# The last feature block of an adapter-conditioned attention and feed-forward layer: its second half leaves as 384 and 128 tokens where it left as 256 and 256

## The chip, the core and the metric

The program runs on one core of one Trainium2 chip. TensorE multiplies matrices (its weight loads are listed apart, as PEld), VectorE (DVE), ScalarE (ACT) and GpSimd (POOL) work on elements, and SyncE (SP) issues most transfers; a transfer issued from SP or ACT runs on the core's 16 DMA engines. Results of TensorE go to PSUM, eight banks of 128 partitions by 512 float32 columns; everything else lives in SBUF. The metric is the time of one execution in microseconds (us), lower is better, given as the median of three runs.

## The reference

32 batch entries of 32 tokens with 256 features, so 1024 tokens. Each batch entry picks one of eight adapters.

```python
x = x + attn(cond(x, itok, weights, fside), W_qkv, b_qkv, W_out, b_out)      # 16 heads of 16, causal
x = x + ffn(cond2(x, Wg, Wu, Wd, Ag, Bg, Au, Bu, Ad, Bd, itok), W1, W2, W3)

# cond2: _lora_linear(x, W, A, B, i) = x @ W + (x @ A[i]) @ B[i], hidden width 1024
h = silu(_lora_linear(x, Wg, Ag, Bg, i)) * _lora_linear(x, Wu, Au, Bu, i)
y = _lora_linear(h, Wd, Ad, Bd, i)

# ffn, hidden width 1024
hidden = silu(y @ W1.T) * (y @ W3.T)
hidden = fwht(hidden)                     # Walsh-Hadamard transform over the 1024
out = hidden @ W2.T                       # 1024 -> 256 features
```

Everything is float32. What the change touches is the last line, `hidden @ W2.T`, and the residual sum behind it.

## The kernel before

Activations are kept with features on the partitions and tokens along the free dimension: 1024 tokens are two halves of 512 (`HT`), and 256 output features are two blocks of 128 (`DC`). A float32 product is made of three fast ones: each operand is split into a high part, rounded to the short-mantissa kind `float32r`, and the rest, `lo`. The helper `both` (lines 480 to 489) issues the three matmuls for one block of 128 by 128 weights: weights high by activations high (L484), weights high by activations low (L486), weights low by activations high (L488). With two tiles given it does each of the three for both of them. Every matmul comes with its own load of 128 columns of weights. Where a small product can do without the split (conditioning, scores, adapters), plain float32 operands are used, in one instruction (L503, L558, L584, L613, L641, L681).

The stages follow each other on TensorE in an order written out by hand: conditioning, attention, the gated adapters' layer ("gate" and "up", then "d0" and "d1"), the feed-forward's two inputs ("f1" and "f3"), and the output product "w2". The Walsh-Hadamard transform has been folded into W2 on the way (`w2_hi`, `w2_lo`), so the last product reads the gated hidden state `h_hi`, `h_lo` directly.

The last stage stands at lines 802 to 813. The list `OUTS` (line 104) says in which pieces the output is made; each entry is (feature block, half of the tokens, first column, last column). The pieces are taken in the groups `[0, 1], [2], [3], [4]`. For a group, TensorE goes over `k`, the eight blocks of 128 hidden features (`HC`), and does the three matmuls of `both` for each, so that a group of one piece is 24 matmuls, each as wide as the piece. Pieces 0 to 2 are full halves of 512 tokens; pieces 3 and 4 share the last half of the last feature block. Each piece has a PSUM bank of its own (`psum_tiles`), freed long before.

When a piece's last matmul is done, VectorE adds the residual to it and writes `tmp_b` (lines 1333 to 1336), and SP, which does nothing else by then, sends that part of `tmp_b` to memory (lines 457 to 460); at the end it waits for all five transfers. Semaphores tie the three together: `full` from TensorE to VectorE, `out_made` from VectorE to SP, `out_stored` from the transfers to SP.

Of the kernel before, what the change touches and what calls it, by code (L numbers as in the profile page):

```python
# [46 lines left out]
HT = TOK // HALVES  # L47
# [53 lines left out]
           + [(PACKED_AT[n] + k * COLS, 1, COLS) for n in (P_D0, P_D1) for k in range(2)]  # L101
           + [(PACKED_AT[P_F + m], 1, COLS) for m in range(HC)])

OUTS = [(0, 0, 0, HT), (0, 1, 0, HT), (1, 0, 0, HT), (1, 1, 0, HT // 2), (1, 1, HT // 2, HT)]
WARM_UP = 14
ALONE = 6
KEEP_WARM = 7
# [21 lines left out]
def psum_tiles():  # L129
# [8 lines left out]
    last = [(a, s, m) for m in range(HC) for a in ("f1", "f3") for s in range(HALVES)]  # L138
    last += [("w2", j, 0) for j in range(len(OUTS))]
    bank_of = dict(plan)  # L140
# [24 lines left out]
def build(nc, index, first, x_slots, w_stream, matrices, w2_t, x_feat, out):  # L165
    with ExitStack() as ctx:
# [219 lines left out]
        def _(sp):  # L386
# [3 lines left out]
            def load_weights(n):  # L390
                if n >= STAGES:
                    wait_weights(sp, n - STAGES)
                at, runs, step = SOURCES[n]
                sp.dma_start(raw[:, n % STAGES, :].rearrange("p (a n) -> p a n", a=runs),
                             w_stream[:, at:at + runs * step].rearrange("p (a n) -> p a n", a=runs)[:, :, 0:COLS // runs])\
                  .then_inc(raw_loaded[n % STAGES], 16)
# [58 lines left out]
            for m in range(HC):  # L455
                load_weights(W_F + m)
            for j, (m, s, c0, c1) in enumerate(OUTS):
                sp.wait_ge(out_made, j + 1)
                sp.dma_start(out[m * P:(m + 1) * P, s * HT + c0:s * HT + c1], tmp_b[:, min(j, 3), c0:c1])\
                  .then_inc(out_stored, 16)  # L460
            sp.wait_ge(out_stored, len(OUTS) * 16)


        @block.tensor
        def _(pe):
# [14 lines left out]
            def both(tiles, w, xs, start, stop):  # L480

                last = []
                for ps, (x_hi, _) in zip(tiles, xs):
                    pe.matmul(ps[:, :], w[0], x_hi, start=start, stop=False)  # L484
                for ps, (_, x_lo) in zip(tiles, xs):
                    pe.matmul(ps[:, :], w[0], x_lo, start=False, stop=False)  # L486
                for ps, (x_hi, _) in zip(tiles, xs):
                    last.append(pe.matmul(ps[:, :], w[1], x_hi, start=False, stop=stop))  # L488
                return last
# [313 lines left out]
            for js in ([0, 1], [2], [3], [4]):  # L803
                tiles = [claim("w2", j, 0) for j in js]
                for k in range(HC):
                    pe.wait_ge(prod_split, ORDINAL["f3", 1, k] + 1)
                    m = OUTS[js[0]][0]
                    w = (w2_hi[:, k, m * P:(m + 1) * P], w2_lo[:, k, m * P:(m + 1) * P])
                    xs = [[h[s][:, k, c0:c1] for h in (h_hi, h_lo)] for _, s, c0, c1 in (OUTS[j] for j in js)]
                    outs = [ps[:, c0:c1] for ps, (_, _, c0, c1) in zip(tiles, (OUTS[j] for j in js))]  # L810
                    last = both(outs, w, xs, k == 0, k == HC - 1)
# [731 lines left out]
```

## Time and profile before

| | us |
|---|---|
| median of 3 runs | 214.09 |
| lowest and highest run | 214.02, 214.77 |
| the profiled execution | 214.37 |
| its span in the trace | 212.6 |
| TensorE busy | 206.2 (97%) |
| VectorE busy | 96.7 (45%) |

The span runs from the first to the last recorded event; the rest of an execution's time, here 1.77 us, lies around it. An engine's busy time counts its own instructions. Matmuls overlap, so the duration of one is longer than the time after which the next one starts; what a row of many matmuls costs is read from their starts. In the trace a plain float32 matmul leaves two matmul records and two load records, a `float32r` one leaves one of each; both kinds are called f32 in the rows, and they are told apart by their line.

### The profile page before, as it was taken

What the parts mean: (1) busy time and instruction counts of PE and PEld (TensorE: products, weight loads), DVE (VectorE), ACT (ScalarE), POOL (GpSimd) and SP (SyncE); (2) the same over time, 40 slices, a digit from 0 to 9 for tenths busy, and PEclk for the clock granted to TensorE, in tenths of its full rate; (3) what the DMA queues carried; (4) which work ended last, traced back from release to release, by engine and by line L of the source; (5) the groups of instructions that cost most, each with busy time, mean ns of one, the idle gap of its engine ahead of it and who ended that gap; (6) DMA issues with size and microseconds to landing.
All of it is one profiled execution on the core that took longest, in us unless ns stands there. A gap on an engine that the chain in (4) does not pass through costs nothing.

```text
span 212.6 us, 5689 instructions
## 1 busy us (share of the span) xinstructions
PE 206.2 (97%) x2265; PEld 164.8 (78%) x2265; DVE 96.7 (45%) x175; ACT 93.1 (44%) x162; POOL 104.9 (49%) x120
## 2 busy tenths in 40 slices
PE   7799999899999999999999999999999999999994
PEld 3467788588777878787888788788888888888894
DVE  3799998897557973020220300067922222220211
ACT  2356889585957042351450460324666664420000
POOL 4005788269656340827643458002599999440000
PEclk9999999999999999999999999999999999999999
DMA  5950056726430362041210451201011000000211
GB/s 152 393 209 3 5 143 159 208 57 173 116 90 15 91 189 74 0 114 24 62 29 23 122 233 33 69 0 33 19 49 54 0 0 0 0 3 0 99 49 49
DMA packets 16265, 16.68 MB, mean 78 GB/s; under 512 B 1776, under 2 KB 13040, under 8 KB 15984
## 3 DMA queue, kind: packets, MB, share of 16 engines
q1 hardware_dynamic: 15808, 15.26, 23.5%
q10 hardware_dynamic: 432, 1.07, 1.6%
q8 instruction: 18, 0.29, 0.6%
q14 instruction: 7, 0.06, 0.1%
HBM read 15.27 MB, written 1.05 MB: 77 GB/s over the span
## 4 chain that ended last, share of the span: by engine, by line
PE 88%; DVE 3%; DMA 3%; ACT 3%; issue 1%; SPq 0%; ACTq 0%
PE bank L484 25%; PE bank L486 23%; PE bank L488 23%; PE bank L641 8%; DMA raw<-w_stream 3%; PE bank L681 2%; DVE aux_lo L1144 1%; PE bank L558 1%; PE bank L584 1%; ACT k_x L843 1%; PE bank L613 1%; PE bank L503 1%; ACT aux_hi L878 1%; PE bank L539 1%; PE bank L538 1%
## 5 line engine op out<-in xcount | busy, mean ns | idle before, releaser
L1391 POOL TENSOR_TENSOR h_lo<-tmp_b,h_hi 128x512 fp32r<-128x512 f32 x32 | 42.6, 1353 | 40.7 <-ACT h_hi L892 40.7
L484 PE MATMUL bank<-act_hi,w_hi 128*128 128x512 f32 x144 | 52.7, 402 | 0.1
L486 PE MATMUL bank<-act_lo,w_hi 128*128 128x512 f32 x144 | 51.1, 391 | 0.0
L488 PE MATMUL bank<-act_hi,w_lo 128*128 128x512 f32 x144 | 50.9, 389 | 0.0
L1214 DVE TENSOR_TENSOR tmp_b<-bank,tmp_a 128x512 f32<-128x512 f32 x32 | 20.7, 684 | 61.7 <-ACT tmp_a L899 35.7
L1344 POOL TENSOR_TENSOR w_lo<-raw,w_hi 128x512 fp32r<-128x512 f32 x21 | 27.0, 1294 | 20.2 <-ACT w_hi L827 20.2
L484 PEld LDWEIGHTS bank<-act_hi,w_hi 128*128 128x128 f32 x144 | 27.0, 188 | 8.1 <-issue 1.9
L899 ACT ACTIVATE tmp_a<-bank 128x512 f32<-128x512 f32 x32 | 17.3, 592 | 33.0 <-PE bank L641 28.8
L488 PEld LDWEIGHTS bank<-act_hi,w_lo 128*128 128x128 f32 x144 | 27.0, 188 | 5.9
L486 PEld LDWEIGHTS bank<-act_lo,w_hi 128*128 128x128 f32 x144 | 27.0, 188 | 5.1
L892 ACT ACTIVATE h_hi<-tmp_b 128x512 fp32r<-128x512 f32 x32 | 19.7, 632 | 19.9 <-DVE tmp_b L1214 19.9
L484 PE MATMUL bank<-h_hi,w_hi 128*128 128x512 f32 (+1 forms) x72 | 22.8, 371 | 0.0
L486 PE MATMUL bank<-h_lo,w_hi 128*128 128x512 f32 (+1 forms) x72 | 22.5, 366 | 0.0
L488 PE MATMUL bank<-h_hi,w_lo 128*128 128x512 f32 (+1 forms) x72 | 22.4, 366 | 0.0
L827 ACT ACTIVATE w_hi<-raw 128x512 fp32r<-128x512 f32 x24 | 14.5, 620 | 9.2 <-DMA raw<-w_stream 8.3
L641 PE MATMUL bank<-z_slots,b_own 64*64 64x128 f32 x512 | 15.8, 272 | 0.1
L486 PEld LDWEIGHTS bank<-h_lo,w_hi 128*128 128x128 f32 x72 | 13.6, 189 | 2.3
L488 PEld LDWEIGHTS bank<-h_hi,w_lo 128*128 128x128 f32 x72 | 13.6, 189 | 2.2
L484 PEld LDWEIGHTS bank<-h_hi,w_hi 128*128 128x128 f32 x72 | 13.3, 189 | 2.5 <-issue 0.3
L641 PEld LDWEIGHTS bank<-z_slots,b_own 64*64 64x64 f32 x512 | 13.9, 132 | 1.7 <-issue 1.4
L1370 POOL COPY a_in<-a_in_raw 128x64 f32 x32 | 6.7, 257 | 13.4 <-DVE w_hi L1060 12.7
L1317 DVE TENSOR_TENSOR act_lo<-bank,act_hi 128x512 fp32r<-128x512 f32 x4 | 2.6, 686 | 19.3 <-ACT act_hi L1006 19.3
(98 smaller groups left out, 252.0 us busy)
## 6 DMA issues: line engine op xcount, KB each, us to landing
raw<-w_stream SPq DMA_DIRECT2D x24, 256.0 KB, 3.5
b_own<-w_stream SPq DMA_DIRECT2D x32, 128.0 KB, 3.0
k_x<-x_slots ACTq DMA_DIRECT2D x2, 512.0 KB, 6.7
resid<-x_feat SPq DMA_DIRECT2D x1, 1024.0 KB, 8.1
tmp_a<-w_t SPq DMA_DIRECT2D x1, 1024.0 KB, 4.8
out_feat<-tmp_b SPq DMA_DIRECT2D x3, 256.0 KB, 2.1
a_down_raw<-w_stream SPq DMA_DIRECT2D x1, 512.0 KB, 3.9
b_down<-w_stream SPq DMA_DIRECT2D x32, 16.0 KB, 2.0
```

Source lines behind the costliest of these rows:

```text
L484: pe.matmul(ps[:, :], w[0], x_hi, start=start, stop=False)
L486: pe.matmul(ps[:, :], w[0], x_lo, start=False, stop=False)
L488: last.append(pe.matmul(ps[:, :], w[1], x_hi, start=False, stop=stop))
L641: ins = pe.matmul(tile(name, s, m)[features, at:at + P], weight(name, s, m, rows_, q)[:, features], slots(name, s, rows_, q).rearrange("p ...
L681: ins = pe.matmul(ps[64 * h + 32 * e:64 * h + 32 * e + 32, (2 * s + q) * 2 * T:(2 * s + q + 1) * 2 * T], a_down[:, m, (s * BH + b) // 2].r ...
L827: act.activation(w_hi[:, at:at + COLS], raw[:, n % STAGES, :], ACT.Copy)\
L892: act.activation(dst, tmp_b[:, ORDINAL[name, s, m] % 4, :], ACT.Copy).then_inc(prod_hi_made, 1)
L899: free(act.activation(tmp_a[:, n % 4, :], tile(name, s, m)[:, :], ACT.Silu), name, s, m)
L1214: free(dve.tensor_tensor(tmp_b[:, ORDINAL[name, s, m] % 4, :], tile(name, s, m)[:, :], tmp_a[:, silus % 4, :], ALU.mult), name, s, m)
L1344: pool.tensor_tensor(w_lo[:, at:at + COLS], raw[:, n % STAGES, :], f32(w_hi[:, at:at + COLS]), ALU.subtract).then_inc(w_lo_made, 1)
L1370: last = pool.tensor_copy(a_in[:, s, :, 2 * i + b // 2, :, b % 2], a_in_raw[:, :, bass.DynSlice(adapter[b], 1), :] .rearrange("p x n r -> ...
L1391: pool.tensor_tensor(lo, tmp_b[:, n % 4, :], f32(hi), ALU.subtract).then_inc(prod_split, 1)
```

## The change

The boundary between the last two pieces moves from column 256 to column 384 of the last half.

```diff
-OUTS = [(0, 0, 0, HT), (0, 1, 0, HT), (1, 0, 0, HT), (1, 1, 0, HT // 2), (1, 1, HT // 2, HT)]
+OUTS = [(0, 0, 0, HT), (0, 1, 0, HT), (1, 0, 0, HT), (1, 1, 0, 3 * HT // 4), (1, 1, 3 * HT // 4, HT)]
```

On TensorE, at the border between piece 3 (in bank1) and piece 4 (in bank3), there stood before:

```order
L484 MATMUL bank1<-h_hi1,w2_hi 128x256
L486 MATMUL bank1<-h_lo1,w2_hi 128x256
L488 MATMUL bank1<-h_hi1,w2_lo 128x256
L484 MATMUL bank3<-h_hi1,w2_hi 128x256
L486 MATMUL bank3<-h_lo1,w2_hi 128x256
L488 MATMUL bank3<-h_hi1,w2_lo 128x256
```

And there stands now:

```order
L484 MATMUL bank1<-h_hi1,w2_hi 128x384
L486 MATMUL bank1<-h_lo1,w2_hi 128x384
L488 MATMUL bank1<-h_hi1,w2_lo 128x384
L484 MATMUL bank3<-h_hi1,w2_hi 128x128
L486 MATMUL bank3<-h_lo1,w2_hi 128x128
L488 MATMUL bank3<-h_hi1,w2_lo 128x128
```

Each bank's three rows stand eight times in a row, once for each block of hidden features, as before; nothing moved, the 24 matmuls of the first piece are wider and the 24 of the last are narrower.

On VectorE, at the program's end, the two last residual sums change their widths:

```order
 L1335 TENSOR_TENSOR tmp_b<-bank,resid 128x512 x3
-L1335 TENSOR_TENSOR tmp_b<-bank,resid 128x256 x2
+L1335 TENSOR_TENSOR tmp_b<-bank,resid 128x384
+L1335 TENSOR_TENSOR tmp_b<-bank,resid 128x128
```

SP's two last transfers change in the same way, from 128 KB each to 192 KB and 64 KB; ScalarE and GpSimd have the same rows.

## Rows read from the trace of the kernel before

**Rows 1.** The page: TensorE's busy time, and its granted clock in 40 slices.

```profile
PE 206.2 (97%) x2265; PEld 164.8 (78%) x2265; DVE 96.7 (45%) x175; ACT 93.1 (44%) x162; POOL 104.9 (49%) x120
PEclk9999999999999999999999999999999999999999
```

**Rows 2.** Chain of waits, 208 us on: start, length, what.

```profile
209.61 0.12 PE bank L486
209.73 0.13 PE bank L488
209.86 0.02 issue
209.89 0.42 DVE tmp_b L1335
```

**Rows 3.** Timeline, last stage: start, length, engine, line, operation, count, idle time before.

```profile
198.50 0.39 PE L484 MATMUL bank<-h_hi,w_hi 128*128 128x512 f32 x1
...
203.94 0.28 PE L484 MATMUL bank<-h_hi,w_hi 128*128 128x256 f32 x1
...
207.01 0.42 DVE L1335 TENSOR_TENSOR tmp_b<-bank,resid 128x256 f32<-128x256 f32 x1 [2.18 <-PE bank L488]
...
209.57 0.28 PE L488 MATMUL bank<-h_hi,w_lo 128*128 128x256 f32 x1
209.89 0.42 DVE L1335 TENSOR_TENSOR tmp_b<-bank,resid 128x256 f32<-128x256 f32 x1 [2.45 <-PE bank L488]
210.34 0.33 SPq L459 DMA_DIRECT2D out_feat<-tmp_b  x1
```

**Rows 4.** Groups by shape, 193 us on: count, busy, mean ns, idle before.

```profile
L488 PE MATMUL bank<-h_hi,w_lo 128*128 128x512 f32 x17 | 6.0, 389 | 0.0
...
L488 PE MATMUL bank<-h_hi,w_lo 128*128 128x256 f32 x16 | 4.5, 283 | 0.0
...
L1335 DVE TENSOR_TENSOR tmp_b<-bank,resid 128x512 f32<-128x512 f32 x3 | 2.0, 687 | 13.9 <-PE bank L488 13.9
L1335 DVE TENSOR_TENSOR tmp_b<-bank,resid 128x256 f32<-128x256 f32 x2 | 0.8, 425 | 4.6 <-PE bank L488 4.6
```

**Rows 5.** Transfers by shape, whole span: count, KB each, median us to landing.

```profile
out_feat<-tmp_b SPq DMA_DIRECT2D x3, 256.0 KB, 2.1
...
b_down<-w_stream SPq DMA_DIRECT2D x32, 16.0 KB, 2.0
...
out_feat<-tmp_b SPq DMA_DIRECT2D x2, 128.0 KB, 1.8
```

**Rows 6.** Weight loads by shape, whole span.

```profile
L641 PEld LDWEIGHTS bank<-z_slots,b_own 64*64 64x64 f32 x512 | 13.9, 132 | 1.7 <-issue 1.4
L488 PEld LDWEIGHTS bank<-h_hi,w_lo 128*128 128x128 f32 x72 | 13.6, 189 | 2.2
...
L681 PEld LDWEIGHTS bank<-tmp_b,a_down 128*32 128x32 f32 x256 | 3.9, 109 | 2.8 <-issue 2.8
...
L699 PEld LDWEIGHTS bank<-warm 128*128 128x128 bf16 x7 | 0.6, 98 | 0.8 <-issue 0.2
```

**Rows 7.** Timeline, TensorE, 16.2 to 17.5 us: conditioning (L503) between two others.

```profile
16.31 1.05 PE L503 MATMUL bank<-prob,k_x 128*128 128x128 f32 x8
17.29 0.39 PE L548 MATMUL bank<-causal_bf,ident_bf 32*128 32x512 bf16 x2
```

**Rows 8.** Groups by shape: conditioning's matmuls (four calls of four) and the adapters' narrow ones.

```profile
L681 PE MATMUL bank<-tmp_b,a_down 128*32 128x64 f32 x256 | 5.2, 222 | 0.0
...
L503 PE MATMUL bank<-prob,k_x 128*128 128x128 f32 x32 | 4.5, 284 | 1.4 <-DVE prob L1051 1.4
```

**Rows 9.** Timeline, TensorE, 120 to 121.2 us: loads and matmuls 32 weight columns wide.

```profile
120.26 0.65 PE L681 MATMUL bank<-tmp_b,a_down 128*32 128x64 f32 x32
```

**Rows 10.** TensorE by stretch: length, busy (count), granted clock, DMA share, GB/s.

```profile
204.10:206.97 2.87, 2.87 (x27) 1.00 0.24 91
206.97:209.86 2.89, 2.88 (x25) 1.00 0.13 45
```

## The prediction

> **What bounds the kernel now.** I read the page first, then the chain of waits at the end, then the timeline of the last stage, and at last groups by shape for the prices. The page says that TensorE is busy for 97% of the span, at the full granted clock in every slice [rows 1]. The chain of waits ends in matmuls, one residual sum on VectorE and the last transfer: the last matmul ends at 209.86 us, the sum takes 0.42, and SP issues the transfer at 210.34 [rows 2, 3]. The span ends at 212.6, so 2.26 us follow that issue. Whatever the change does to the last 48 matmuls or to the sum and transfer behind them is therefore on the path; nothing else in the program changes.
>
> What one matmul costs in a row of them is read from starts, not from durations. The 24 of piece 2, 512 columns wide, start at 198.50 and the first 256-wide one starts at 203.94 [rows 3]: 5.44 / 24 = 0.2267 us each. The 48 that are 256 wide start from 203.94 to 209.57: 5.63 / 47 = 0.1198 us each. The granted clock is 1.00 in that stretch [rows 10], so the higher of the two levels, 2.4 GHz, at which 512 and 256 columns are 0.2133 and 0.1067 us. Both widths leave the same rest, 0.0133 us. So at these widths a matmul costs its columns plus 0.013, and the 384-wide ones should cost 0.160 + 0.0133 = 0.1733 us. No row shows one of this kind (L484, L486, L488) under 256 columns, and that is what the forecast turns on.
>
> **The change part by part.**
>
> Piece 3, 24 matmuls of 384: 24 x 0.1733 = 4.16 us, interpolated between two measured widths; I see no more than 0.02 of error here.
>
> Piece 4, 24 matmuls of 128: unknown spacing c. From the first matmul of piece 3 to the end of the last of piece 4 it is 4.16 + 23c + the last one's duration. Durations are 389 ns at 512 and 283 at 256 [rows 4], which on a line gives 230 at 128. Before, the same stretch is 5.63 + 0.283 = 5.91. So TensorE's end moves by 4.16 + 23c + 0.23 - 5.91 = 23c - 1.52.
> The lower bound is columns plus the rest, 0.0533 + 0.0133 = 0.067: nothing is gained or lost (+0.01). It can't go under that by any row.
> The upper bound is the spacing of plain float32 matmuls of the same shape. Conditioning's 16 instructions leave 32 records [rows 8], and eight records run from 16.31 to the next matmul at 17.29 [rows 7] or, leaving out the last one's duration, (1.05 - 0.27) / 7 = 0.111 a record, 0.222 an instruction: +3.59.
> Between them stands the weight load. Every matmul here brings 128 new columns of weights. Loads of 32, 64 and 128 float32 columns last 109, 132 and 189 ns [rows 6], so each further column costs (189 - 132) / 64 = 0.89 ns between the last two and 0.72 between the first two; at 0.8 to 0.89 a full load holds its path for 102 to 114 ns, twice as long as 128 columns of activations take. A load can be hidden under one matmul before it, and at 256 columns (0.107 streaming) that just fits; at 128 it does not, and the load sets the pace. The nearest rows agree: full float32 loads of 128 columns come 0.111 us apart at the densest [rows 7], and the same lines at 256 columns 0.12 [rows 3]. No full load stands closer to its neighbour anywhere. I take c = 0.12, the spacing of the same lines with the same loads; narrowing the activations from 256 to 128 then saves nothing. That is 23 x 0.12 - 1.52 = +1.24 us. With 0.111 it is +1.03, with 0.114 + 0.0133 = 0.127 it is +1.40.
>
> The Trainium skill bears on this in "TensorE: Matmul & The Clock Gate", section "LDWEIGHTS (loading the stationary operand)": a load takes its number of weight columns divided by 1.2 GHz, and its table of perf modes leaves FP32 out of the fast load. An estimate from that page is 107 ns for 128 columns, 0.107 to 0.12 a matmul, +0.94 to +1.24. The trace agrees in slope, 0.72 to 0.89 ns a column, and shows a bf16 load at 98 ns against 189.
>
> The sum behind piece 3: 0.56 us for 384 columns on the line between 687 and 425 ns [rows 4]. Its bank is full at about 208.3, it is done by 208.9, and piece 4's matmuls cover it until 211.1. Its transfer of 192 KB is issued then and lands at about 2.0 us [rows 5], before the last one is issued at about 211.4. Cost nothing; without that cover it would be at most its own 0.56, but even at c = 0.067 TensorE ends 1.5 us after piece 3.
>
> The sum behind piece 4: 425 - (687 - 425) / 2 = 294 ns for 128 columns instead of 425: -0.13 us. The bounds are 0 and -0.21 (half of 425).
>
> The last transfer: 256 KB land after 2.1 us and 128 KB after 1.8, but loads of 16 KB take 2.0 [rows 5], so size is only a part of it. On the slope 64 KB would save 0.15, flat it saves nothing; I take -0.06. SP and VectorE have nothing else queued there.
>
> The sum is +1.24 - 0.13 - 0.06 = +1.05 us. Against the profiled execution, 214.37 with a span of 212.6 and 1.77 around it, that is 215.42, span 213.65. That execution was 0.28 above the median of 214.09, inside the runs' 214.02 to 214.77; for the median I forecast 215.1.
>
> **The rivals.**
>
> *Streaming alone sets the pace (c = 0.067).* For it: at 512 and 256 columns the time is columns plus 0.0133 to within a nanosecond, with no sign of a load. And loads of 32 columns come every (0.65 - 0.22) / 31 = 14 ns [rows 8, 9], 0.43 ns a column, which would make 56 ns of a full one. Against it: those loads go to different column groups and may run side by side, and 256 columns are just wide enough to hide 107 to 114 ns. Then it is 0.01 - 0.13 - 0.06 = -0.18, so 213.9: not slower, the shorter tail is all that is left.
> The same page, section "Back-to-back issue gap", gives 81 ns a matmul for streams of load and matmul at 128 columns. By that estimate the sum is 23 x 0.081 - 1.52 - 0.19 = +0.15, 214.2; no row here shows such a spacing.
>
> *A short `float32r` matmul falls back to the rate of plain float32.* Then 128 columns cost as conditioning's do, 0.222 us, and the end moves by +3.59 - 0.19 = +3.4: 217.5. If each costs as a 512-wide one, 0.2267, with 0.389 for the last, it is 217.8. For it: every fast matmul in this trace is 256 or wider and every narrower one is plain float32, so no row rules it out. Against it: the rest of 0.0133 us is the same at 512 and 256, and a rate that depends on width leaves no trace in it. It decides from any c above 0.15 on.
>
> *The tail gives more than TensorE takes.* The sum and the transfer would have to fall by over 1.2 us together; their bounds are 0.21 and 0.15. Not with c = 0.12.
>
> **How the numbers follow.** The load sets the pace: 0.52, at 215.1, its own range 214.8 (c = 0.111, transfer -0.15) to 215.5. Streaming alone or nearly: 0.20, 213.9 to 214.3. Plain float32 rate: 0.25, 217.4 to 217.8. The last 0.03 lies between or outside. The range is 213.8 to 217.7: the likeliest case and the dear one inside, and most of the cheap one.
> About 0.5%, 1.07 us, is what a measurement of this kernel can tell from no change. The likeliest case sits on that line, and I give it half to each side: within 0.5% it is 0.27 + 0.17 from streaming = 0.44, slower 0.25 + 0.25 + 0.02 = 0.52, faster 0.04.
>
> **What would show it.** In the changed kernel's timeline, starts of 384-wide matmuls 0.173 apart, those of the last 24 at 0.12 (right), 0.067 or 0.08 (streaming), 0.22 (plain rate). The last sum lasting 0.29 us, and the end of the span 2.2 us after the last issue. I am wrong in the likeliest case if the spacing is under 0.10 or over 0.14, or if the stages before piece 3 move by over 0.1 us.

## The result and the profile after

The changed kernel takes 214.97 us (median of 6 runs, 214.65 to 215.11) against 214.25 (6 runs, 214.02 to 214.77); the ratio is 1.0029, with a 95% interval of 1.0015 to 1.0042. That is 0.6 us slower, clear of noise and inside the 0.5% that counts here as no difference. In the profiled execution the span is 213.3 us, 0.7 more.

The end of the chain of waits, answering [rows 2]; columns are start, length, what:

```profile
208.15 0.17 PE bank L488
208.32 0.06 PE bank L484
208.38 0.11 PE bank L486
208.50 0.11 PE bank L488
...
210.84 0.13 PE bank L488
210.99 0.29 DVE tmp_b L1335
```

The chain is built as before: matmuls to the end, one sum, one transfer. Only its steps have changed: 0.17 us a matmul, then one of 0.06, then 0.11. The timeline, answering [rows 3], shows the starts themselves and the weight loads beside them:

```profile
203.98 0.33 PE L484 MATMUL bank<-h_hi,w_hi 128*128 128x384 f32 x1
...
207.99 0.33 PE L488 MATMUL bank<-h_hi,w_lo 128*128 128x384 f32 x1
207.99 0.19 PEld L484 LDWEIGHTS bank<-h_hi,w_hi 128*128 128x128 f32 x1
208.16 0.22 PE L484 MATMUL bank<-h_hi,w_hi 128*128 128x128 f32 x1
208.16 0.19 PEld L486 LDWEIGHTS bank<-h_lo,w_hi 128*128 128x128 f32 x1
208.22 0.27 PE L486 MATMUL bank<-h_lo,w_hi 128*128 128x128 f32 x1
208.27 0.19 PEld L488 LDWEIGHTS bank<-h_hi,w_lo 128*128 128x128 f32 x1
208.33 0.27 PE L488 MATMUL bank<-h_hi,w_lo 128*128 128x128 f32 x1
208.36 0.56 DVE L1335 TENSOR_TENSOR tmp_b<-bank,resid 128x384 f32<-128x384 f32 x1 [3.49 <-PE bank L488]
208.38 0.19 PEld L484 LDWEIGHTS bank<-h_hi,w_hi 128*128 128x128 f32 x1
...
210.68 0.28 PE L488 MATMUL bank<-h_hi,w_lo 128*128 128x128 f32 x1
210.99 0.29 DVE L1335 TENSOR_TENSOR tmp_b<-bank,resid 128x128 f32<-128x128 f32 x1 [2.07 <-PE bank L488]
211.31 0.33 SPq L459 DMA_DIRECT2D out_feat<-tmp_b  x1
```

While 384 columns stream, each load starts with a matmul and the next waits for the next matmul. From 208.16 on the loads follow each other every 0.11 us, and the matmuls come with them. From 208.22 to 210.68 there are 22 gaps, 0.1118 us each; streaming 128 columns is 0.053. Only the first gap, 0.06, is short: the load of the first narrow matmul had stood under the last wide one. That matmul lasts 0.22 us, the others, which wait for their loads, 0.27 to 0.28.

The transfers, answering [rows 5]; count, KB each, median us to landing:

```profile
out_feat<-tmp_b SPq DMA_DIRECT2D x3, 256.0 KB, 2.1
out_feat<-tmp_b SPq DMA_DIRECT2D x1, 192.0 KB, 1.9
out_feat<-tmp_b SPq DMA_DIRECT2D x1, 64.0 KB, 1.6
```

| from the two timelines, us | before | after | moved |
|---|---|---|---|
| first matmul of piece 3 starts | 203.94 | 203.98 | +0.04 |
| from there to the end of the last matmul | 5.91 | 6.98 | +1.07 |
| the last sum | 0.42 | 0.29 | -0.13 |
| last transfer issued to the end of the span | 2.26 | 1.99 | -0.27 |
| span | 212.6 | 213.3 | +0.7 |

The stages before piece 3 end where they did in this pair. In other profiles they end up to 0.6 us earlier (e_w64) or 0.4 later (e_w64_t256), so below single profiles are compared from the first matmul of piece 3 on: before, 212.6 - 203.94 = 8.66 us to the end of the span; after, 9.32.

### The profile page after: what moved, and what is told of

The parts are those of the page before. It is cut to its first block, busy times and chain, and to the rows that moved or that the text cites. A ratio compares the mean times of both kernels' runs of the same rounds, so it can differ in the third digit from the quotient of the medians.

```text
span 213.3 us, 5689 instructions
## 1 busy us (share of the span) xinstructions
PE 207.1 (97%) x2265; PEld 165.8 (78%) x2265; DVE 97.0 (45%) x175; ACT 93.1 (44%) x162; POOL 104.6 (49%) x120
## 3 DMA queue, kind: packets, MB, share of 16 engines
q10 hardware_dynamic: 432, 1.07, 1.7%
HBM read 15.27 MB, written 1.05 MB: 77 GB/s over the span
## 4 chain that ended last, share of the span: by engine, by line
PE 88%; DMA 3%; DVE 3%; ACT 3%; issue 1%; SPq 0%; ACTq 0%
PE bank L484 25%; PE bank L486 23%; PE bank L488 23%; PE bank L641 8%; DMA raw<-w_stream 3%; PE bank L681 2%; DVE aux_lo L1144 1%; PE bank L584 1%; PE bank L558 1%; ACT k_x L843 1%; PE bank L613 1%; PE bank L503 1%; ACT aux_hi L878 1%; PE bank L539 1%; PE bank L538 1%
## 5 line engine op out<-in xcount | busy, mean ns | idle before, releaser
L484 PE MATMUL bank<-h_hi,w_hi 128*128 128x512 f32 (+2 forms) x72 | 23.1, 375 | 0.0
L486 PE MATMUL bank<-h_lo,w_hi 128*128 128x512 f32 (+2 forms) x72 | 22.8, 371 | 0.0
L488 PE MATMUL bank<-h_hi,w_lo 128*128 128x512 f32 (+2 forms) x72 | 22.8, 371 | 0.0
L1335 DVE TENSOR_TENSOR tmp_b<-bank,resid 128x512 f32<-128x512 f32 (+2 forms) x5 | 2.8, 583 | 19.4 <-PE bank L488 19.4
```

## The experiments

**Is it the load, or the streaming of a short operand?** Half-rate streaming under 256 columns would also give about 0.11 us at 128. First the boundary at column 448:

```diff
-(1, 1, 0, HT // 2), (1, 1, HT // 2, HT)]
+(1, 1, 0, 448), (1, 1, 448, HT)]
```

> The boundary is put at column 448: 24 matmuls of 448 columns, then 24 of 64. Theory, the weight load sets the pace: a load of 128 columns holds its path for 0.112 us whatever streams, so the 64-wide matmuls start 0.112 us apart, exactly as the 128-wide ones did; the 448-wide ones 0.200 apart. From the first 448-wide start to the last end 4.80 + 23 x 0.112 + 0.27 = 7.65 us against 5.91 before, +1.7; the last sum 0.22 us (-0.20) and its 32 KB transfer 1.5 us (-0.3), together +1.2 us. Rival, a short moving operand is streamed at half rate: 64 columns at 1.2 GHz are 0.053 + 0.005 = 0.058 us apart, the stretch is 6.4 us, +0.5, and with the tail the kernel is level with the one before (0.0 us).

Measured: ratio 1.0064 (1.0043 to 1.0084), 8.66 us become 9.83. TensorE's starts and durations:

```profile
203.97 0.36 PE L484 MATMUL bank<-h_hi,w_hi 128*128 128x448 f32 x1
...
208.83 0.19 PE L484 MATMUL bank<-h_hi,w_hi 128*128 128x64 f32 x1
208.86 0.28 PE L486 MATMUL bank<-h_lo,w_hi 128*128 128x64 f32 x1
208.97 0.28 PE L488 MATMUL bank<-h_hi,w_lo 128*128 128x64 f32 x1
...
211.32 0.28 PE L488 MATMUL bank<-h_hi,w_lo 128*128 128x64 f32 x1
```

(211.32 - 208.86) / 22 = 0.1118 us, the same as with twice the columns, to the 0.0005 us that two printed starts can tell. How much is streamed does not matter any more; the half-rate rival is out. The very first gap, 0.03 us, is what 64 columns cost when the load was already done. The 448-wide ones are 0.2025 apart (4.86 / 24), not 0.200.

Then the changed kernel with half of the weights' columns in the last piece, the same activations streamed (64 of that piece's 128 output features are left out):

```diff
+                    if js == [4]:
+                        w, outs = tuple(x[:, 0:P // 2] for x in w), [o[0:P // 2] for o in outs]
```

> The changed kernel, but the last piece's 24 matmuls use only 64 of the 128 weight columns (64 of the 128 output features of that piece are left out); they stream 128 columns of activations as before. Theory, the weight load sets the pace: a load of 64 columns holds its path for 0.056 us, under the 0.067 of streaming, so the spacing falls from 0.112 to 0.067, TensorE's end comes about 1.0 us earlier than in the changed kernel, and the kernel is 0.3 us faster than the one before (0.1 if the change of tile shape costs one exposed load of 0.2). Rival, half-rate streaming of a short operand: the width streamed is unchanged, so the spacing stays at 0.112 and the time at +0.7 us over before.

```profile
207.49 0.22 PE L484 MATMUL bank<-h_hi,w_hi 128*64 128x128 f32 x1
207.55 0.22 PE L486 MATMUL bank<-h_lo,w_hi 128*64 128x128 f32 x1
...
208.87 0.22 PE L488 MATMUL bank<-h_hi,w_lo 128*64 128x128 f32 x1
```

1.38 / 23 = 0.060 us: halving the loaded columns halves the spacing, with the streamed ones as they were. The output's partitions are halved too, but they don't hold the pace: the first gap of 0.03 us in e_448_64 stands behind a matmul with all 128 of them, whose load was done. From the start of piece 3 (203.31) to the span's end (211.5) it is 8.19 us, 1.1 less than in the changed kernel. The ratio to before is 0.999 (0.9975 to 1.0005): an interval that holds the 0.3 us gained that were expected, and no change. No exposed load showed at the change of tile shape. The spacing is even below the 0.067 expected, so the rest of 0.0133 us that the prediction took as fixed is not fixed.

Two more kernels with the same halved weights, at 64 tokens (boundary at 448) and at 256 (the boundary of before), separate the two limits. Of each there is a single execution, the profiled one, so they say something of spacings and nothing of times:

> Pieces of 448 and 64 tokens, the last with 64 of its 128 weight columns (64 output features of it are left out). Theory, a load holds its path for a time in proportion to its weight columns, 0.112 us for 128: 64-column loads are 0.056 apart and set the pace again, since streaming 64 columns takes only 0.030 (the gap between the first two 64-wide matmuls of the run at column 448). Rival, a fixed floor of a load of its own, or of issuing a matmul: the spacing of 0.060 that 64-column loads showed with 128 tokens would have to be something else than streaming, and the spacing here could be anything from 0.030 to 0.060; below 0.050 the theory of proportion falls.

> The kernel before, 256 and 256 tokens, with 64 of 128 weight columns in the last piece (64 output features of it are left out). Streaming sets the pace in any theory; the run asks what the rest of 0.013 us on top of the streamed columns is. If it belongs to the streaming of a float32r matmul, it stays, 0.120 us apart. If it goes with the columns loaded beside it, it halves as it did with 128 tokens (0.060 = 0.0533 + 0.0067), 0.113 apart.

64 tokens first, then 256:

```profile
208.67 0.22 PE L486 MATMUL bank<-h_lo,w_hi 128*64 128x64 f32 x1
...
209.95 0.22 PE L488 MATMUL bank<-h_hi,w_lo 128*64 128x64 f32 x1
```

```profile
207.25 0.28 PE L484 MATMUL bank<-h_hi,w_hi 128*64 128x256 f32 x1
...
209.86 0.28 PE L488 MATMUL bank<-h_hi,w_lo 128*64 128x256 f32 x1
```

1.28 / 22 = 0.058 us at 64 tokens: half of 0.1118 plus 0.002, so the load's time goes with its columns. 2.61 / 23 = 0.1135 at 256: the rest fell from 0.013 to 0.007, so it isn't a fixed part of streaming 256 columns. Halving the weight columns halves the output's partitions too, and these runs don't part the two. One row of before does in part, the bf16 matmuls of L699, at a granted clock of 1.00:

```profile
10.50 0.59 PE L699 MATMUL bank<-warm 128*128 128x512 bf16 x2
...
11.58 0.38 PE L699 MATMUL bank<-warm 128*128 128x512 bf16 x1
```

They have 128 weight columns and 128 output partitions and start 1.08 / 5 = 0.216 us apart, a rest of 0.003, with loads that last 98 ns [rows 6]. So 128 output partitions alone don't cost 0.013; whether it is the load or the kind of operand stays open. Spacings in us, from the timelines of these runs (those of 240 and 272 columns from e_272_240b below):

| streamed columns | 128 weight columns | 64 weight columns | columns / 2.4 GHz |
|---|---|---|---|
| 64 | 0.1118 | 0.058 | 0.027 |
| 128 | 0.1118 | 0.060 | 0.053 |
| 240 | 0.111 | | 0.100 |
| 256 | 0.120 | 0.1135 | 0.107 |
| 272 | 0.125 | | 0.113 |
| 384 | 0.174 | | 0.160 |
| 448 | 0.2025 | | 0.187 |
| 512 | 0.227 | | 0.213 |

From 256 columns on, the rest with 128 weight columns lies between 0.012 (272) and 0.016 (448, the same in e_448_64 and e_w64_t64); it is not one constant. Why 448 costs the most is open.

**How far ahead does a load run?** The two last pieces in one group, so that wide and narrow matmuls alternate:

```diff
-            for js in ([0, 1], [2], [3], [4]):
+            for js in ([0, 1], [2], [3, 4]):
```

> The changed kernel with pieces 3 and 4 in one group, so that 384-wide and 128-wide matmuls alternate. Theory, one load ahead at most: the load behind a 384-wide matmul is hidden, the load behind a 128-wide one is not, a pair costs 0.173 + 0.112 = 0.285 us and TensorE's end is the changed kernel's within 0.05. Rival, loads can run further ahead: a wide matmul gives its slack to the next load too, a pair costs 0.173 + 0.067 = 0.240 us and TensorE ends 1.1 us earlier, level with the kernel before. In both the two sums (0.56 and 0.29 us) now stand behind each other at the end, so the tail is about 0.45 us longer than the changed kernel's: +1.3 us over before by the theory, +0.2 by the rival.

Timeline; each row is one wide and one narrow matmul:

```profile
204.13 0.30 PEld L486 LDWEIGHTS bank<-h_lo,w_hi 128*128 128x128 f32 x2
...
204.19 0.45 PE L486 MATMUL bank<-h_lo,w_hi 128*128 128x384 f32 x2
204.41 0.30 PEld L488 LDWEIGHTS bank<-h_hi,w_lo 128*128 128x128 f32 x2
...
210.49 0.45 PE L488 MATMUL bank<-h_hi,w_lo 128*128 128x384 f32 x2
210.92 0.76 DVE L1335 TENSOR_TENSOR tmp_b<-bank,resid 128x384 f32<-128x384 f32 x2 [6.07 <-PE bank L488]
211.50 0.81 SPq L459 DMA_DIRECT2D out_feat<-tmp_b  x2
```

22 pairs in 6.30 us are 0.286 each, 0.174 + 0.112: one load ahead, and the slack under a wide matmul is lost. The loads show it: the two of a row start 0.11 us apart (0.30 less the 0.19 that one lasts), and then 0.17 pass, a whole wide matmul, before the next row's. TensorE's stretch is 6.98 us, that of the changed kernel. The tail grew by more than I had sized: the two transfers are issued 0.48 us apart (0.81 less one issue of 0.33), and SP issues the second 0.3 us after its sum has ended, where the last issue of the changed kernel came 0.03 us after. 9.32 us became 10.14. The ratio is 1.0082 (1.0058 to 1.0105), about 1.8 us where 1.3 was expected.

**What is the tail worth alone?** TensorE as before, the last sum and transfer cut to 128 columns (128 tokens of the last piece are left out):

```diff
+                c0 = 3 * HT // 4 if j == 4 else c0
```

(once in SP's loop ahead of the transfer, once in VectorE's ahead of the sum)

> The kernel before, 256 and 256 columns on TensorE, but the last sum and the last transfer take only the last 128 columns (128 tokens of the last piece are left out). Both theories: TensorE's spacing stays 0.120, and only the tail's gain is seen: the sum 0.29 instead of 0.42 us, the transfer of 64 KB 1.6 instead of 1.8, -0.3 us in all, ratio 0.9985. If the kernel gains nothing, the shorter tail was worth nothing and the changed kernel's +0.7 us is all that TensorE lost.

Ratio 0.9978 (0.9965 to 0.9992), 0.5 us; in the profile 8.66 us become 8.28, so -0.38: 0.13 in the sum and 0.25 behind the last issue (210.29 to 212.3). Both are more than the 0.3 expected, which the interval (0.2 to 0.75 us) still holds; it is clear of no change.

**The same matmuls, the other tail.** 128 columns first, 384 last:

```diff
-(1, 1, 0, HT // 2), (1, 1, HT // 2, HT)]
+(1, 1, 0, HT // 4), (1, 1, HT // 4, HT)]
```

> The same two widths in the other order: 128 columns first, 384 last. On TensorE it is the same 48 matmuls, so its end should move by the same +1.1 us as in the changed kernel (24 x 0.112 + 23 x 0.173 + 0.34 = 7.0 us against 5.91). The tail goes the other way: the last sum takes 0.56 us (+0.13 over before) and the last transfer of 192 KB 1.9 (+0.1), so +1.3 us over before. Theory that the tail matters as sized: this run is about 0.6 us slower than the changed kernel. Rival, only TensorE's end matters: the same +0.7 as the changed kernel.

Ratio 1.0049 (1.0029 to 1.0068), 1.0 us where 1.3 was expected; from piece 3 to the end 9.95 us, 0.63 more than the changed kernel, as expected. TensorE's stretch is 7.05 us. The rival, that only TensorE's end matters, falls by the profile; the two ratios' intervals overlap and would not settle it alone.

**Where does the threshold lie, and is there a better boundary?** Pieces of 272 and 240:

```diff
-(1, 1, 0, HT // 2), (1, 1, HT // 2, HT)]
+(1, 1, 0, 272), (1, 1, 272, HT)]
```

> The boundary at column 272: 24 matmuls of 272 columns and 24 of 240. Theory, the load sets the pace only under about 237 columns (0.112 - 0.0133 = 0.0987 us at 2.4 GHz): the spacings are 0.1267 and 0.1133, their sum 0.240 as before, TensorE's end moves by under 0.02 us, the tail gives 0.02; no difference to the kernel before. Rival, a threshold at 256 columns below which the rate halves: 240 columns are 0.200 + 0.005 us apart, TensorE ends 2.2 us later.

Ratio 0.9989 (0.9976 to 1.0002). Since that interval reaches from a gain of 0.2% to none, it was run again:

> The kernel with the boundary at column 272 once more, in more rounds, since its first interval holds no difference as well as 0.2% gained. Theory: 0.00 to -0.08 us against before (TensorE's stretch measured 0.05 us shorter, the last sum 0.02), ratio 0.9996 to 1.0, not to be told from no change. If the ratio is 0.999 or below with an interval clear of 1, something beside the last stage differs.

Ratio 0.9997 (0.9983 to 1.0012). The 240-wide matmuls in that run:

```profile
206.92 0.27 PE L484 MATMUL bank<-h_hi,w_hi 128*128 128x240 f32 x1
...
209.48 0.28 PE L488 MATMUL bank<-h_hi,w_lo 128*128 128x240 f32 x1
```

2.56 / 23 = 0.111 us, already at the load's pace; no cliff at 256 columns. From piece 3 on the profile is 0.17 us shorter than before, of which 0.07 is TensorE's; the runs can't tell it from no change.

Last, no boundary at all: `(1, 1, 0, HT)` as the only entry and `([0, 1], [2], [3])` as the groups.

> The last half in one piece of 512 columns, no boundary. TensorE saves 24 times the rest of 0.0133 us: 23 x 0.2267 + 0.389 = 5.60 us against 5.91, -0.31. The tail grows: the last sum 0.69 instead of 0.42 us (+0.26) and the last transfer of 256 KB 2.1 instead of 1.8 (+0.3). Together +0.25 us over before. If the transfer's size counts for nothing, it is -0.05.

Ratio 1.0004 (0.9989 to 1.0018). TensorE's last start is at 209.29, 23 x 0.2267 after piece 3's first, and the stretch 5.60 us, as expected; the last sum takes 0.69, and 2.46 us follow the last issue. All together +0.16 where +0.25 was expected: by this profile the boundary at 256 buys in the tail what it costs on TensorE, and a little more; by the runs the two can't be told apart. No version here that computes the whole output beats the kernel before by what can be measured.

## Why the prediction was right

Forecast was 215.1 us and +1.05; measured are 214.97 and, by the ratio, +0.6 (0.3 to 0.9). Its likeliest case, that the weight load sets the pace, is what happened, shown by e_448_64 and e_w64: the mechanism was right, the size 0.4 us too large. That 214.97 is so near to 215.1 is partly luck, since the forecast started from 214.09 and the kernel before measured 214.25 beside the changed one. Its terms:

- *The 384-wide matmuls*, 0.1733 us: measured 4.18 / 24 = 0.174.
- *The spacing c*, 0.12: measured 0.112. Over 23 gaps that is 0.24 us less, 0.06 of it from the short first gap, which was not in the sum. I took the row of the same lines at 256 columns, which was limited by streaming plus its rest. The dense loads of conditioning [rows 7], 0.111, were the better price: they were at the load's own limit.
- *The last matmul's duration*, 230 ns by a line through 512 and 256 columns: measured 275. A matmul that waits for its load lasts longer than the 0.22 of the first one, which doesn't. So TensorE's end moved by 1.07 us instead of 1.24.
- *The sum behind piece 4*, 294 ns: measured 291. *The sum behind piece 3*, 0.56, was hidden; TensorE ended over 2 us later.
- *The last transfer*, -0.06: this was sized wrong. Its landing went from 1.8 to 1.6 us and the whole stretch behind the issue from 2.26 to 1.99. I had leaned on the 2.0 us of 16 KB loads [rows 5], transfers in the other direction. A line through the two stores alone, 2.1 and 1.8, gives 1.65 for 64 KB, and the experiments follow it roughly: 1.9 for 224 and 192 KB, 1.6 for 64, 1.5 for 32. Only where the two were issued 0.48 us apart (e_pair) did they take 2.0 and 1.8. With -0.27 the sum is +1.07 - 0.13 - 0.27 = +0.67, plus 0.04 from before piece 3, the 0.7 of the spans.
- *The rivals*: streaming alone had rested on loads of 32 columns 14 ns apart [rows 9]. They go to different column groups; a full load goes at 0.87 ns a column. Why theirs are faster no run here separates. The fall to plain float32 rate did not happen at 240, 128 or 64 columns.

On the weight load the Trainium skill ("TensorE: Matmul & The Clock Gate", section "LDWEIGHTS (loading the stationary operand)") says that a load takes its columns divided by 1.2 GHz; an estimate from that is 107 ns for 128 columns and 53 for 64. The measured spacings of 112 and 58 agree with 5 ns on top. Its 81 ns a matmul at 128 columns (section "Back-to-back issue gap") does not hold for these float32r matmuls: 112.

The chance of no difference was put at 0.44 and that of slower at 0.52; the likeliest case, at +1.05, lay on the line of 1.07 between them and was split in half. So the side that came was the less likely one by a little. Two mis-sized terms in the same direction, 0.17 us on TensorE and 0.21 in the last transfer, put the measured time on it.

## What to carry to other kernels

A matmul with its own 128 float32 weight columns costs 0.112 us however little it streams. Cutting an output into pieces to shorten the tail costs TensorE 0.3 us for the 24 matmuls more (e_whole). As soon as a piece is narrower than some 240 columns it costs about 10 ns more for each column less (24 matmuls at 2.4 GHz, whose columns move to the other piece): 112 columns less are 1.1 us, and 1.07 was measured. A column less in the last sum and transfer gave back 3 ns (0.40 us for 128). To price a step that the profile doesn't show, look for the row that is held by the same resource, not for the one with the same line number.

## What had not been expected of the hardware

Loads do not pool their slack: behind a 384-wide matmul the next load still waits for the next start (0.286 us a pair). And what a float32r matmul costs beyond its columns is not fixed: 0.013 us with 128 weight columns and 0.007 with 64, at 256 streamed, and 0.003 for the bf16 matmuls of L699. That it goes with the load beside it fits all three and is not shown; by what mechanism was not tried.
